# Attention block on one core: the output projection is evicted and added to x by one VectorE instruction

## The chip, the cores and the metric

The kernel is written in Bass for Trainium2 and runs on one core of one chip. The metric is the device time of one execution in microseconds (us). The kernel before takes 413.24 us, the median of 3 runs (413.13 to 413.28).

## What is computed

x has shape (4, 256, 32, 32): 4 images, 256 channels, 1024 pixels. Per image:

```
x_n = group_norm(x, gn_w, gn_b)                # 32 groups of 8 channels
q, k, v = conv1x1(x_n; wq,bq), conv1x1(x_n; wk,bk), conv1x1(x_n; wv,bv)
attn = softmax(q k^T * 64**-0.5)               # 4 heads of 64 channels, 1024 x 1024
out  = conv1x1(attn v; wp, bp)
return x + out
```

The change concerns the last two lines: the projection, its bias bp, and the addition of x.

## The kernel before

Each engine has its own instruction list, written out by hand; semaphores join them. An image is 32 slots (4 heads, 2 halves of the queries, 4 pairs of key tiles); the counter G runs over the 128 slots of four images and 13 more behind them (the tail). `place(G)` gives the image b and its slot g. Operands of full precision are split into two f16 parts, `hi` and `lo`.

In slot G, TensorE (PE) does `scores(G)` (two key tiles into one of two double banks st0, st1), two `maximum` matmuls for a later unit (banks mx0, mx1 in turn), at most one job of the table `JOBS`, and `weigh(G-4)`, the 24 products with v in bank pv. All jobs share one bank, `gen`. Before a job writes it, `bank_empty` waits until the job before has been evicted. The jobs are k, q, v (projections of the normalised image), o (transposes of the attention output), y (the output projection, one of four quarters: channel half i, pixel half j), mean and var (group statistics).

```
JOBS = {0: ("k", 1, 1, 0), 1: ("y", 0, 0, -1), 2: ("q", 1, 1, 0), 3: ("y", 1, 0, -1), 4: ("mean", 0, 0, 1),
        5: ("o", 1, 1, -1), 7: ("y", 0, 1, -1), 8: ("var", 0, 0, 1), 9: ("y", 1, 1, -1), 10: ("v", 1, 0, 0), ...}
TAIL_JOBS = {0: ("y", 0, 0, -1), 2: ("y", 1, 0, -1), 4: ("o", 1, 1, -1), 5: ("y", 0, 1, -1), 6: ("y", 1, 1, -1)}
```

The last number is the image relative to b: the y jobs of an image run in slots 1, 3, 7 and 9 of the next one, and those of image 3 in the tail. The first image thus has no y job, and the last has no mean and no var job. Where a long job (k, q, v, y) falls into a slot with the transpose of the maxima (every slot g with g mod 4 = 2), `early` puts it ahead of that transpose and of the first maximum.

What the other engines do in slot G:

- ScalarE (ACT): `exponent(G)`, two passes over the scores (L628 to p_hi, L631 to the full value), and behind it the eviction of the job of slot G. For y that is L617: scale, bias bp, into y32, and it raises s_y.
- VectorE (DVE), in this order: `normalise` (L717, L718) where g mod 4 = 0, `p_low(G-1)` (L711) for even G-1, `row_out` (L693) where g mod 4 = 2, the two row maxima (L681) with the low part of a v or o job (L705) around them, `join_max` (L686) where g mod 4 = 1, and the channel statistics of the next image (L727, L728) in slots 0 and 2 (1 and 3 in image 0). In the tail it also does `residual` (L735), in the slot behind that of the y job.
- GpSimd (POOL): the hi and lo parts of k and q (L853, L289), `p_low(G-1)` (L863) for odd G-1, and up to slot 128 the `residual` of the y job of slot G-1 (L858), which adds xres (a second load of x) to y32.
- The SP queue issues the loads, the copies of k and q to their operand tiles, the row of maxima (L325), the load of xres in slot 27 (L349) and the stores (L330), which wait for s_yx, raised by `residual`.

Of the kernel before, what the change touches and what calls it, by code (L numbers as in the profile page):

```python
# [12 lines left out]
def attention_block(nc, x, gn_w, gn_b, wq, bq, wk, bk, wv, bv, wp, bp, out):  # L13
# [55 lines left out]
    with ctx:  # L69
# [120 lines left out]
        s_pv = sem("s_pv")  # L190
        s_o32 = sem("s_o32")

        s_y = sem("s_y")
        s_yx = sem("s_yx")
        s_out = sem("s_out")
        s_ones = sem("s_ones")
# [198 lines left out]
        def _(pe):  # L395
            held = []

            def bank_empty():

                if not held:  # L400
                    return
                kind, i, j, b = held.pop()
                if kind in "kq":
                    wait(pe, s_e32[kind], nth(i, j, b) + 1)
                elif kind in "vo":
                    wait(pe, s_lo[kind], nth(i, j, b) + 1)
                elif kind == "y":
                    wait(pe, s_y, 4 * b + i + 2 * j + 1)
                else:
                    wait(pe, {"mean": s_gmean, "var": s_gvar}[kind], b + 1)  # L410

# [8 lines left out]
            def job(kind, i, j, b, bank=gen):  # L420
                if kind in "kqv":
                    wait_z(pe, b, j)
                if kind == "mean":
                    wait(pe, s_mv, b + 1)
                if kind == "var":
                    wait(pe, s_dev, b + 1)
                if kind == "o":
                    wait(pe, s_o32, UNITS * b + 4 * i + 2 * j + 2)
                if kind == "y":
                    wait(pe, s_lo["o"], nth(1, j, b) + 1)  # L430
                if bank is gen:
                    bank_empty()
                half = halves(j)
                o = slice(i * P, (i + 1) * P)
                if kind in "kq":
                    for mm in parts(bank[:, :], lambda t: (w_hi[kind][:, t, o], w_lo[kind][:, t, o]),
                                    lambda t: (z_hi[:, t, half], z_lo[:, t, half])):
                        last = mm
                if kind == "v":
                    for c in range(4):  # L440
                        k = slice((4 * j + c) * P, (4 * j + c + 1) * P)
                        for mm in parts(bank[:, c * P:(c + 1) * P], lambda t: (z_hi[:, t, k], z_lo[:, t, k]),
                                        lambda t: (w_hi["v"][:, t, o], w_lo["v"][:, t, o]), first=c == 0):
                            last = mm
                if kind == "y":
                    for mm in parts(bank[:, :], lambda t: (w_hi["p"][:, t, o], w_lo["p"][:, t, o]),
                                    lambda t: (oT_hi[:, t, half], oT_lo[:, t, half])):
                        last = mm
                if kind == "o":
                    for q in range(QT):  # L450
                        last = nc.tensor.transpose(bank[:, q * P:(q + 1) * P], o32[:, j, q, :], ident[:, :])  # L451
                if kind == "mean":
                    last = nc.tensor.matmul(bank[:, 0:CT], group_avg[:, :], mv[:, :, 0], start=True, stop=True)
                if kind == "var":
                    last = nc.tensor.matmul(bank[:, 0:CT], group_avg[:, :], dev2[:, :], start=True, stop=True)
                last.then_inc(s_gen_full, 1)
                if bank is gen:
                    held.append((kind, i, j, b))

# [131 lines left out]
        def _(act):  # L591
# [9 lines left out]
                act.wait_ge(s_gen_full, filled[0])  # L601

            def job(kind, i, j, b, bank=gen):
                bank_full()
                if kind in "kq":
                    wait(act, s_lo[kind], nth(i, j, b) - 1)
                    nc.scalar.activation(e32[kind][:, j, :], bank[:, :], ACT.Identity, bias=bias_s[kind][:, i:i + 1],  # L607
                                         scale=QKV_SCALE / (Z_SCALE * W_SCALE)).then_inc(s_e32[kind], 1)
                if kind == "v":
                    nc.scalar.activation(v_rows(v_hi, i, j), bank[:, :].rearrange("p (n d) -> p n d", d=D), ACT.Copy,  # L610
                                         scale=QKV_SCALE / (Z_SCALE * W_SCALE)).then_inc(s_hi["v"], 1)
                if kind == "o":
                    nc.scalar.activation(oT_hi[:, i, halves(j)], bank[:, :], ACT.Identity, bias=bv_o[:, i:i + 1])\
                      .then_inc(s_hi["o"], 1)
                if kind == "y":
                    wait(act, s_out, 64 * b)
                    nc.scalar.activation(y32[:, i, halves(j)], bank[:, :], ACT.Identity,  # L617
                                         bias=vec["p"][:, i:i + 1], scale=1.0 / (O_SCALE * W_SCALE)).then_inc(s_y, 1)
                if kind == "mean":
                    nc.scalar.activation(gmean[:, :], bank[:, 0:CT], ACT.Copy).then_inc(s_gmean, 1)  # L620
                if kind == "var":
                    nc.scalar.activation(gvar[:, :], bank[:, 0:CT], ACT.Copy).then_inc(s_gvar, 1)
# [50 lines left out]
        def _(dve):  # L673
# [55 lines left out]
                if t == CT - 1:  # L729
                    ins.then_inc(s_mv, 1)  # L730

            def residual(i, j, b):
                wait(dve, s_y, 4 * b + i + 2 * j + 1)
                wait(dve, s_xres, 16 * (b + 1))
                nc.vector.tensor_tensor(y32[:, i, halves(j)], y32[:, i, halves(j)], xres[:, i, halves(j)], ALU.add)\  # L735
                  .then_inc(s_yx, 1)

            def slot(G):
                b, g = place(G)
# [3 lines left out]
                    normalise(old // SPU)  # L743
                done, top = shift_at(G), maxima_at(G)
                early = done is not None and long_at(G)
                if slot_of(G - 1) is not None and lo_on_dve(G - 1):
                    p_low(G - 1)
                U, n = top or (None, None)
                todo = job_at(G - 1)
                if early and todo and todo[0] in "vo":  # L750
                    low(*todo)
                if done is not None:
# [2 lines left out]
                    row_max(U, n)  # L755
                if not early and todo and todo[0] in "vo":
                    low(*todo)
                if todo and todo[0] == "y" and G > TOTAL:
                    residual(*todo[1:])
                if top:  # L760
                    row_max(U, n + 1)
                if top and n == 2 * QT - 2:
# [65 lines left out]
        def _(pool):  # L828
# [23 lines left out]
                    wait(pool, s_mx_full, MXJ + 4)  # L852
                nc.gpsimd.tensor_copy(kq_hi[kind][:, halves(j)], e32[kind][:, j, :]).then_inc(s_hi[kind], 1)  # L853

            def residual(i, j, b):
                wait(pool, s_y, 4 * b + i + 2 * j + 1)
                wait(pool, s_xres, 16 * (b + 1))
                nc.gpsimd.tensor_tensor(y32[:, i, halves(j)], y32[:, i, halves(j)], xres[:, i, halves(j)], ALU.add)\  # L858
                  .then_inc(s_yx, 1)

            def p_low(G):
                wait(pool, s_exp, G + 1)
# [3 lines left out]
            def slot(G):  # L866
# [4 lines left out]
                    low_kq(pool, *todo)  # L871
                if slot_of(G - 1) is not None and not lo_on_dve(G - 1):
                    p_low(G - 1)
                if todo and todo[0] == "y" and G <= TOTAL:
                    residual(*todo[1:])
                if todo and todo[0] == "mean":
                    about_group_mean(pool, b + 1)
                if todo and todo[0] == "var":
                    norm_factors(b + 1)
                if b + 1 < B and g in (14, 15):  # L880
                    z_low(pool, b + 1, g - 14)

            nc.gpsimd.memset(ident[:, :], 0.0).then_inc(s_cfill, 1)
            nc.gpsimd.memset(group_avg[:, :], 1.0 / GROUP).then_inc(s_cfill, 1)
# [53 lines left out]
```

## Time and profile before

| | before |
|---|---|
| median of 3 runs | 413.24 us |
| profiled execution | 414.99 us |
| its span | 413.3 us |
| mean granted TensorE clock | 0.986 |
| TensorE matmul busy | 378.1 us, 91% |
| VectorE busy | 313.4 us, 76% |
| ScalarE busy | 313.4 us, 76% |
| GpSimd busy | 232.1 us, 56% |

The span is the profiled program from its first to its last instruction or transfer; the profiled execution's time has 1.7 us more around it. A busy share is an average over all stages. In the timeline, the first number is an instruction's start in us from the start of the span and the second its duration; a bracket tells how long the engine had been idle and whose work ended that.

### The profile page before, as it was taken

Reading aid. Unit: us, or ns where it says so; the run is one execution under the profiler, and the core shown is the slowest. Engines: PE = TensorE matmul, PEld = TensorE weight load, DVE = VectorE, ACT = ScalarE, POOL = GpSimd, SP = SyncE. Lnnn points to the kernel's source line nnn. Section 1 sums busy time; section 2 is a strip of 40 time slices with the busy share of each in tenths; the row PEclk is TensorE's granted clock in tenths of the full one; section 3 lists DMA queues with packets and bytes.
Section 4 is the critical chain, followed back from the end, with each engine's and each line's share of the span. In section 5 each row is a group of like instructions: output and inputs, shape, how many; then the busy total and the mean of one; then the engine's idle time right before and its main releaser. Section 6 shows DMA issues by size and latency. Waiting matters only on the chain.

```text
span 413.3 us, 11152 instructions
## 1 busy us (share of the span) xinstructions
PE 378.1 (91%) x4653; PEld 234.8 (57%) x4653; DVE 313.4 (76%) x536; ACT 313.4 (76%) x366; POOL 232.1 (56%) x195
## 2 busy tenths in 40 slices
PE   2789899899999999799999999799999999999884
PEld 1524476456665567456665657456665656655661
DVE  4776979678877987767878987757887687998552
ACT  1526787987878777988787787978778787888851
POOL 5144754776277665677476666478455744344440
PEclk9998999999999999999999999989999999999997
DMA  6054500034300611034320621003320351000301
GB/s 204 0 117 140 135 22 2 18 112 96 113 26 2 156 52 52 2 103 104 71 84 2 141 67 52 2 2 79 78 103 2 72 136 52 2 2 2 105 34 69
DMA packets 14409, 26.97 MB, mean 65 GB/s; under 512 B 2444, under 2 KB 4248, under 8 KB 14360
## 3 DMA queue, kind: packets, MB, share of 16 engines
q1 hardware_dynamic: 14336, 26.26, 22.9%
q8 instruction: 37, 0.61, 0.6%
q14 instruction: 12, 0.10, 0.1%
q10 hardware_dynamic: 24, 0.01, 0.0%
HBM read 9.44 MB, written 4.19 MB: 33 GB/s over the span
## 4 chain that ended last, share of the span: by engine, by line
PE 71%; DVE 15%; ACT 5%; issue 5%; DVEq 1%; POOLq 1%; POOL 1%
PE gen L417 17%; PE st L487 11%; PE st L488 10%; PE mx L465 10%; PE pv L505 6%; PE pv L508 6%; PE pv L507 6%; DVE mx L681 5%; DVE p_lo L711 4%; PE st L417 2%; ACT st L631 2%; DVEq L676 1%; DVE shift_row L693 1%; PE gen L451 1%; PE mx L472 1%
## 5 line engine op out<-in xcount | busy, mean ns | idle before, releaser
L863 POOL TENSOR_TENSOR p_lo<-p,p_hi 128x1024 f16<-128x1024 f32 x64 | 136.2, 2128 | 101.4 <-ACT p L631 101.4
L681 DVE TENSOR_REDUCE mx<-mx 128x1 f32<-128x512 f32 x256 | 171.3, 685 | 22.3 <-PE mx L465 19.6
L628 ACT ACTIVATE p_hi<-st 128x1024 f16<-128x1024 f32 x128 | 131.0, 1024 | 64.6 <-PE st L488 63.1
L505 PE MATMUL pv<-v_hi,p_hi 128*128 128x65 f16 x1024 | 106.1, 194 | 2.1 <-DVE o L718 1.8
L507 PE MATMUL pv<-v_lo,p_hi 128*128 128x64 f16 x1024 | 106.2, 193 | 0.0
L508 PE MATMUL pv<-v_hi,p_lo 128*128 128x65 f16 x1024 | 106.2, 194 | 0.0
L487 PE MATMUL st<-q_twice,k_both 128*128 128x512 f16 x256 | 97.6, 381 | 6.3 <-DVE p_lo L711 6.3
L505 PEld LDWEIGHTS pv<-v_hi,p_hi 128*128 128x128 f16 x1024 | 94.6, 98 | 12.0 <-issue 4.0
L507 PEld LDWEIGHTS pv<-v_lo,p_hi 128*128 128x128 f16 x1024 | 93.9, 98 | 13.2
L488 PE MATMUL st<-q_max,k_one 65*128 65x512 f16 x256 | 97.7, 382 | 0.0
L508 PEld LDWEIGHTS pv<-v_hi,p_lo 128*128 128x128 f16 x1024 | 94.0, 98 | 0.0
L465 PE MATMUL mx<-k_both,q_twice 128*128 128x512 f16 x244 | 87.8, 381 | 4.7 <-DVE shift_row L693 2.7
L711 DVE TENSOR_TENSOR p_lo<-st,p_hi 128x1024 f16<-128x1024 f32 x64 | 77.7, 1215 | 18.7 <-ACT st L631 18.5
L631 ACT ACTIVATE st<-st 128x1024 f32<-128x1024 f32 x64 | 65.3, 1021 | 0.0
L631 ACT ACTIVATE p<-st 128x1024 f32<-128x1024 f32 x64 | 65.3, 1020 | 0.0
L465 PEld LDWEIGHTS mx<-k_both,q_twice 128*128 128x128 f16 x244 | 24.2, 99 | 34.6 <-DVE shift_row L693 8.5
L487 PEld LDWEIGHTS st<-q_twice,k_both 128*128 128x128 f16 x256 | 25.2, 99 | 24.7 <-issue 5.8
L488 PEld LDWEIGHTS st<-q_max,k_one 65*128 65x128 f16 x256 | 25.1, 98 | 17.0 <-issue 0.3
L693 DVE TENSOR_SCALAR shift_row<-mx 4x128 f16<-4x128 f32 x32 | 8.9, 277 | 30.8 <-PE mx L472 30.8
L853 POOL CAST st_hi_k<-e_k 128x512 f16<-128x512 f32 x16 | 9.8, 610 | 32.0 <-ACT e_k L607 22.1
L417 PE MATMUL gen<-w_hi_v,z_lo 128*128 128x128 f16 x128 | 23.4, 225 | 0.0
L417 PE MATMUL gen<-w_lo_v,z_hi 128*128 128x128 f16 x128 | 23.4, 225 | 0.0
(140 smaller groups left out, 491.6 us busy)
## 6 DMA issues: line engine op xcount, KB each, us to landing
xres<-in_x_dram SPq DMA_DIRECT2D x4, 1024.0 KB, 5.0
out_dram<-y SPq DMA_DIRECT2D x16, 256.0 KB, 2.2
q_twice<-st_hi_q SPq DMA_DIRECT2D x28, 128.0 KB, 2.3
xin<-in_x_dram SPq DMA_DIRECT2D x6, 512.0 KB, 3.3
k_both<-st_hi_k SPq DMA_DIRECT2D x16, 128.0 KB, 2.3
k_one<-st_hi_k SPq DMA_DIRECT2D x16, 128.0 KB, 2.4
k_both<-st_lo_k SPq DMA_DIRECT2D x16, 128.0 KB, 2.3
q_max<-st_lo_q SPq DMA_DIRECT2D x14, 128.0 KB, 2.4
```

What stands on the lines that cost most here:

```text
L417: yield nc.tensor.matmul(dst, a, c, start=first and t == 0 and n == 0, stop=t == CT - 1 and n == 2, skip_group_check=True)
L465: nc.tensor.matmul(mxb[(MXJ * U + j) % 2][:, :], q_twice[:, head, q:q + P], k_both[:, head, halves(part)], start=True, stop=True).then_inc ...
L487: nc.tensor.matmul(dst, k_both[:, head, k], q_twice[:, head, q], start=True, stop=False)
L488: last = nc.tensor.matmul(dst, k_one[:, head, k], q_max[:, head, q], start=False, stop=True)
L505: nc.tensor.matmul(pv_v[:, q, :], hi, vh, start=k == 0 and q == 0, stop=False, skip_group_check=True)
L507: nc.tensor.matmul(pv_v[:, q, 0:D], hi, vl, start=False, stop=False, skip_group_check=True)
L508: last = nc.tensor.matmul(pv_v[:, q, :], lo, vh, start=False, stop=k == NK - 1, skip_group_check=True)
L628: nc.scalar.activation(p_hi[:, G % PR, :, :], scores, ACT.Exp, scale=SM_SCALE / M_SCALE)
L631: nc.scalar.activation(p_full(G), scores, ACT.Exp, scale=SM_SCALE / M_SCALE).then_inc(s_exp, 1)
L681: nc.vector.reduce_max(mx8[:, U % 2, tile, part:part + 1], mxb[(MXJ * U + j) % 2][:, :], AX.X)\
L711: nc.vector.tensor_tensor(p_lo[:, G % PR, :, :], p_full(G), p_hi[:, G % PR, :, :], ALU.subtract)\
L863: nc.gpsimd.tensor_tensor(p_lo[:, G % PR, :, :], p_full(G), p_hi[:, G % PR, :, :], ALU.subtract)\
```

## The change

ScalarE no longer evicts y jobs, and they no longer raise s_gen_full but a semaphore of their own, s_y_full. On VectorE `finish` takes the place of `residual`: one scalar_tensor_tensor reads the bank and xres, computes bank * scale + xres, writes y32 and raises s_yx. It stands in the slot behind that of the y job, for all 16 quarters, ahead of `p_low`, `row_out` and the maxima and behind `normalise`. TensorE's `bank_empty` waits for s_yx instead of s_y. On GpSimd `residual` goes, and `add_bias` adds bp to xres in place, 128 x 1024 elements each in slots 29 and 31 of every image. The load of xres stays where it is.

```diff
--- before.py
+++ after.py
@@ -190,7 +190,8 @@
         s_pv = sem("s_pv")
         s_o32 = sem("s_o32")
 
-        s_y = sem("s_y")
+        s_y_full = sem("s_y_full")
+        s_xb = sem("s_xb")
         s_yx = sem("s_yx")
         s_out = sem("s_out")
         s_ones = sem("s_ones")
@@ -405,7 +406,7 @@
                 elif kind in "vo":
                     wait(pe, s_lo[kind], nth(i, j, b) + 1)
                 elif kind == "y":
-                    wait(pe, s_y, 4 * b + i + 2 * j + 1)
+                    wait(pe, s_yx, 4 * b + i + 2 * j + 1)
                 else:
                     wait(pe, {"mean": s_gmean, "var": s_gvar}[kind], b + 1)
 
@@ -453,7 +454,7 @@
                     last = nc.tensor.matmul(bank[:, 0:CT], group_avg[:, :], mv[:, :, 0], start=True, stop=True)
                 if kind == "var":
                     last = nc.tensor.matmul(bank[:, 0:CT], group_avg[:, :], dev2[:, :], start=True, stop=True)
-                last.then_inc(s_gen_full, 1)
+                last.then_inc(s_y_full if kind == "y" else s_gen_full, 1)
                 if bank is gen:
                     held.append((kind, i, j, b))
 
@@ -601,6 +602,8 @@
                 act.wait_ge(s_gen_full, filled[0])
 
             def job(kind, i, j, b, bank=gen):
+                if kind == "y":
+                    return
                 bank_full()
                 if kind in "kq":
                     wait(act, s_lo[kind], nth(i, j, b) - 1)
@@ -612,10 +615,6 @@
                 if kind == "o":
                     nc.scalar.activation(oT_hi[:, i, halves(j)], bank[:, :], ACT.Identity, bias=bv_o[:, i:i + 1])\
                       .then_inc(s_hi["o"], 1)
-                if kind == "y":
-                    wait(act, s_out, 64 * b)
-                    nc.scalar.activation(y32[:, i, halves(j)], bank[:, :], ACT.Identity,
-                                         bias=vec["p"][:, i:i + 1], scale=1.0 / (O_SCALE * W_SCALE)).then_inc(s_y, 1)
                 if kind == "mean":
                     nc.scalar.activation(gmean[:, :], bank[:, 0:CT], ACT.Copy).then_inc(s_gmean, 1)
                 if kind == "var":
@@ -729,11 +728,14 @@
                 if t == CT - 1:
                     ins.then_inc(s_mv, 1)
 
-            def residual(i, j, b):
-                wait(dve, s_y, 4 * b + i + 2 * j + 1)
-                wait(dve, s_xres, 16 * (b + 1))
-                nc.vector.tensor_tensor(y32[:, i, halves(j)], y32[:, i, halves(j)], xres[:, i, halves(j)], ALU.add)\
-                  .then_inc(s_yx, 1)
+            def finish(i, j, b, bank):
+
+                wait(dve, s_y_full, 4 * b + i + 2 * j + 1)
+                wait(dve, s_xb, CT * b + i + 1)
+                wait(dve, s_out, 64 * b)
+                nc.vector.scalar_tensor_tensor(out=y32[:, i, halves(j)], in0=bank[:, :],
+                                               scalar=1.0 / (O_SCALE * W_SCALE), in1=xres[:, i, halves(j)],
+                                               op0=ALU.mult, op1=ALU.add).then_inc(s_yx, 1)
 
             def slot(G):
                 b, g = place(G)
@@ -743,10 +745,12 @@
                     normalise(old // SPU)
                 done, top = shift_at(G), maxima_at(G)
                 early = done is not None and long_at(G)
+                todo = job_at(G - 1)
+                if todo and todo[0] == "y":
+                    finish(*todo[1:], tail_bank(G - 1))
                 if slot_of(G - 1) is not None and lo_on_dve(G - 1):
                     p_low(G - 1)
                 U, n = top or (None, None)
-                todo = job_at(G - 1)
                 if early and todo and todo[0] in "vo":
                     low(*todo)
                 if done is not None:
@@ -755,8 +759,6 @@
                     row_max(U, n)
                 if not early and todo and todo[0] in "vo":
                     low(*todo)
-                if todo and todo[0] == "y" and G > TOTAL:
-                    residual(*todo[1:])
                 if top:
                     row_max(U, n + 1)
                 if top and n == 2 * QT - 2:
@@ -852,11 +854,10 @@
                     wait(pool, s_mx_full, MXJ + 4)
                 nc.gpsimd.tensor_copy(kq_hi[kind][:, halves(j)], e32[kind][:, j, :]).then_inc(s_hi[kind], 1)
 
-            def residual(i, j, b):
-                wait(pool, s_y, 4 * b + i + 2 * j + 1)
+            def add_bias(b, i):
                 wait(pool, s_xres, 16 * (b + 1))
-                nc.gpsimd.tensor_tensor(y32[:, i, halves(j)], y32[:, i, halves(j)], xres[:, i, halves(j)], ALU.add)\
-                  .then_inc(s_yx, 1)
+                nc.gpsimd.tensor_scalar(xres[:, i, :], xres[:, i, :], vec["p"][:, i:i + 1], None, ALU.add)\
+                  .then_inc(s_xb, 1)
 
             def p_low(G):
                 wait(pool, s_exp, G + 1)
@@ -871,14 +872,14 @@
                     low_kq(pool, *todo)
                 if slot_of(G - 1) is not None and not lo_on_dve(G - 1):
                     p_low(G - 1)
-                if todo and todo[0] == "y" and G <= TOTAL:
-                    residual(*todo[1:])
                 if todo and todo[0] == "mean":
                     about_group_mean(pool, b + 1)
                 if todo and todo[0] == "var":
                     norm_factors(b + 1)
                 if b + 1 < B and g in (14, 15):
                     z_low(pool, b + 1, g - 14)
+                if b < B and g in (29, 31):
+                    add_bias(b, (g - 29) // 2)
 
             nc.gpsimd.memset(ident[:, :], 0.0).then_inc(s_cfill, 1)
             nc.gpsimd.memset(group_avg[:, :], 1.0 / GROUP).then_inc(s_cfill, 1)
```

On VectorE, the piece from the maxima of slot 1 to slot 4 of the image behind the first one (y is y32, mx is a mx bank or mx8), before:

```order
L681 TENSOR_REDUCE mx<-mx 128x1 x2
L686 TENSOR_REDUCE mx<-mx 128x4
L693 TENSOR_SCALAR shift_row<-mx 4x128
L681 TENSOR_REDUCE mx<-mx 128x1 x2
L727 BN_STATS bn<-xin 128x6 x2
L728 BN_AGGR mv<-bn 128x2
L711 TENSOR_TENSOR p_lo<-st,p_hi 128x1024
L681 TENSOR_REDUCE mx<-mx 128x1 x2
L717 RECIPROCAL rden<-pv 128x4
L718 TENSOR_TENSOR o<-pv,rden 128x4x64
L681 TENSOR_REDUCE mx<-mx 128x1 x2
```

and now:

```order
L680 TENSOR_REDUCE mx<-mx 128x1 x2
L685 TENSOR_REDUCE mx<-mx 128x4
L736 SCALAR_TENSOR_TENSOR y<-gen,xres 128x512
L692 TENSOR_SCALAR shift_row<-mx 4x128
L680 TENSOR_REDUCE mx<-mx 128x1 x2
L726 BN_STATS bn<-xin 128x6 x2
L727 BN_AGGR mv<-bn 128x2
L710 TENSOR_TENSOR p_lo<-st,p_hi 128x1024
L680 TENSOR_REDUCE mx<-mx 128x1 x2
L716 RECIPROCAL rden<-pv 128x4
L717 TENSOR_TENSOR o<-pv,rden 128x4x64
L736 SCALAR_TENSOR_TENSOR y<-gen,xres 128x512
```

The first `L736` stands between the joined maxima of slot 1 and the shift_row of slot 2, the second behind o, ahead of the maxima of slot 4.

```order
L680 TENSOR_REDUCE mx<-mx 128x1 x2
L716 RECIPROCAL rden<-pv 128x4
L717 TENSOR_TENSOR o<-pv,rden 128x4x64
L736 SCALAR_TENSOR_TENSOR y<-gen,xres 128x512
L680 TENSOR_REDUCE mx<-mx 128x1 x2
L710 TENSOR_TENSOR p_lo<-st,p_hi 128x1024
L680 TENSOR_REDUCE mx<-mx 128x1 x2
L685 TENSOR_REDUCE mx<-mx 128x4
L736 SCALAR_TENSOR_TENSOR y<-gen,xres 128x512
```

This is the same list on VectorE at slots 8 to 10 now: the third `L736` follows o, the fourth the joined maxima.

On GpSimd, slots 29 to 31 of image 0 and the first three slots behind them, before:

```order
L853 CAST st_hi_q<-e_q 128x512
L289 TENSOR_TENSOR st_lo_q<-e_q,st_hi_q 128x512
L863 TENSOR_TENSOR p_lo<-p,p_hi 128x1024 x2
L853 CAST st_hi_k<-e_k 128x512
L289 TENSOR_TENSOR st_lo_k<-e_k,st_hi_k 128x512
L863 TENSOR_TENSOR p_lo<-p,p_hi 128x1024
L858 TENSOR_TENSOR y<-y,xres 128x512
L853 CAST st_hi_q<-e_q 128x512
L289 TENSOR_TENSOR st_lo_q<-e_q,st_hi_q 128x512
```

and now:

```order
L855 CAST st_hi_q<-e_q 128x512
L290 TENSOR_TENSOR st_lo_q<-e_q,st_hi_q 128x512
L859 TENSOR_SCALAR xres<-xres,vec_cols 128x1024
L864 TENSOR_TENSOR p_lo<-p,p_hi 128x1024
L859 TENSOR_SCALAR xres<-xres,vec_cols 128x1024
L864 TENSOR_TENSOR p_lo<-p,p_hi 128x1024
L855 CAST st_hi_k<-e_k 128x512
L290 TENSOR_TENSOR st_lo_k<-e_k,st_hi_k 128x512
L864 TENSOR_TENSOR p_lo<-p,p_hi 128x1024
L855 CAST st_hi_q<-e_q 128x512
```

Two passes over xres have come in, one ahead of each p_lo, and the two residual additions have gone.

## Rows read from the trace of the kernel before

**Rows 1.** The page, busy time of each engine, share of the span, instructions.

```profile
PE 378.1 (91%) x4653; PEld 234.8 (57%) x4653; DVE 313.4 (76%) x536; ACT 313.4 (76%) x366; POOL 232.1 (56%) x195
```

**Rows 2.** Timeline, ScalarE, VectorE, TensorE around slot 2 of image 1; start, duration.

```profile
130.21 0.69 ACT L617 ACTIVATE y<-gen,vec_cols 128x512 f32<-128x512 f32 x1
...
131.45 0.16 DVE L686 TENSOR_REDUCE mx<-mx 128x4 f32<-128x8 f32 x1
133.12 0.28 DVE L693 TENSOR_SCALAR shift_row<-mx 4x128 f16<-4x128 f32 x1 [1.52 <-PE mx L472]
...
131.52 0.38 PE L417 MATMUL gen<-z_hi,w_hi_q 128*128 128x512 f16 x1
```

**Rows 3.** Groups by line and form: count, busy time, mean ns, idle before.

```profile
L863 POOL TENSOR_TENSOR p_lo<-p,p_hi 128x1024 f16<-128x1024 f32 x64 | 136.2, 2128 | 101.4 <-ACT p L631 101.4
...
L858 POOL TENSOR_TENSOR y<-y,xres 128x512 f32<-128x512 f32 x12 | 15.2, 1266 | 0.0
...
L705 DVE SCALAR_TENSOR_TENSOR oT_lo<-gen,bv_o,oT_hi 128x512 f16<-128x512 f32 x16 | 11.9, 743 | 2.7 <-ACT oT_hi L613 2.7
...
L705 DVE SCALAR_TENSOR_TENSOR v_lo<-gen,v_hi 128x512 f16<-128x512 f32 x16 | 10.9, 681 | 2.6 <-ACT v_hi L610 2.6
...
L853 POOL CAST st_hi_k<-e_k 128x512 f16<-128x512 f32 x16 | 9.8, 610 | 32.0 <-ACT e_k L607 22.1 <-SPq L387 9.9
```

**Rows 4.** Timeline, VectorE and TensorE, slots 3 and 4 of image 1.

```profile
136.55 1.17 DVE L711 TENSOR_TENSOR p_lo<-st,p_hi 128x1024 f16<-128x1024 f32 x1
...
139.08 0.42 DVE L718 TENSOR_TENSOR o<-pv,rden 128x256 f32<-128x256 f32 x1
139.42 1.28 DVE L681 TENSOR_REDUCE mx<-mx 128x1 f32<-128x512 f32 x2
...
137.87 0.38 PE L487 MATMUL st<-q_twice,k_both 128*128 128x512 f16 x1 [0.28 <-DVE p_lo L711]
...
138.95 0.28 PE L453 MATMUL gen<-mv,group_avg 128*128 128x2 f32 x2
```

**Rows 5.** Timeline, VectorE and TensorE, slots 8 to 10 of image 1.

```profile
149.04 0.42 DVE L718 TENSOR_TENSOR o<-pv,rden 128x256 f32<-128x256 f32 x1
...
154.28 0.16 DVE L686 TENSOR_REDUCE mx<-mx 128x4 f32<-128x8 f32 x1
...
149.67 0.28 PE L455 MATMUL gen<-dev,group_avg 128*128 128x2 f32 x2
...
154.95 0.22 PE L417 MATMUL gen<-w_hi_v,z_hi 128*128 128x128 f16 x1
```

**Rows 6.** Timeline, VectorE, slot 1 of image 2.

```profile
225.96 0.16 DVE L686 TENSOR_REDUCE mx<-mx 128x4 f32<-128x8 f32 x1
```

**Rows 7.** Timeline, VectorE and TensorE, slots 1, 2, 9 and 10 of image 3.

```profile
321.19 0.16 DVE L686 TENSOR_REDUCE mx<-mx 128x4 f32<-128x8 f32 x1
...
344.04 0.16 DVE L686 TENSOR_REDUCE mx<-mx 128x4 f32<-128x8 f32 x1
...
321.86 0.38 PE L417 MATMUL gen<-z_hi,w_hi_q 128*128 128x512 f16 x1
...
344.71 0.22 PE L417 MATMUL gen<-w_hi_v,z_hi 128*128 128x128 f16 x1
```

**Rows 8.** Timeline, VectorE and ScalarE, the tail.

```profile
397.95 2.14 DVE L735 TENSOR_TENSOR y<-y,xres 128x512 f32<-128x512 f32 x1 [0.61 <-ACT y L617]
...
410.14 0.69 DVE L735 TENSOR_TENSOR y<-y,xres 128x512 f32<-128x512 f32 x1 [1.44 <-ACT y L617]
...
409.42 0.69 ACT L617 ACTIVATE y<-st,vec_cols 128x512 f32<-128x512 f32 x1 [1.45 <-PE st L417]
```

**Rows 9.** Timeline, GpSimd, slots 30 and 32 of image 0 (p_lo of 29 and 31).

```profile
119.99 2.12 POOL L863 TENSOR_TENSOR p_lo<-p,p_hi 128x1024 f16<-128x1024 f32 x1 [0.37 <-ACT p L631]
124.93 2.13 POOL L863 TENSOR_TENSOR p_lo<-p,p_hi 128x1024 f16<-128x1024 f32 x1 [2.81 <-ACT p L631]
```

**Rows 10.** The page, DMA issues: count, KB each, median us to landing.

```profile
xres<-in_x_dram SPq DMA_DIRECT2D x4, 1024.0 KB, 5.0
```

## The prediction

> **What bounds the kernel now.** I read the busy times first: TensorE's matmuls fill 91% of the span, VectorE and ScalarE 76% each, GpSimd 56% [rows 1]. By these averages, 0.7 us moved from ScalarE to VectorE now and then is neutral. But TensorE sets the pace: VectorE waits for it at slot 2 with all its work done [rows 2], and GpSimd idles 101.4 us for ScalarE, which has its scores from TensorE [rows 3]. So what counts is whether TensorE gets its bank back in time. I therefore went to the timeline around each y job and asked two things: when does TensorE want bank gen again, and when will VectorE have emptied it?
>
> Around slot 2 of image 1 [rows 2] ScalarE evicts y from 130.21 to 130.90, and TensorE starts the next job in gen, q, at 131.52. So there are 0.62 us to spare. VectorE ends its joined maxima at 131.61 and then sits idle for 1.52 us until TensorE's transpose arrives. That idle time looks like cover, but it isn't: the transpose stands behind the q job on TensorE, and the q job will now wait for VectorE.
>
> **What the eviction costs on VectorE.** No row before shows the new instruction. The nearest has the same operation, a PSUM bank and an SBUF tile as inputs, 512 elements and a constant scale: the low part of v, 681 ns; the form with a scale per partition takes 743 ns [rows 3]. I take 0.68 us and keep 0.74 for the range.
>
> From VectorE's end to TensorE's start I take 0.15 us: p_lo ends at 136.55 + 1.17 = 137.72, and TensorE, which waited for it, starts at 137.87 [rows 4]. A following VectorE instruction starts some 0.08 us ahead of the profiled end of the one before it: o ends at 139.50, the maxima start at 139.42 [rows 4].
>
> **The waits, one by one, image 1.** In each, the new instruction starts 0.08 us ahead of the end of its predecessor, takes 0.68, and TensorE follows 0.15 later.
>
> - Slot 2: predecessor is the joined maximum, end 131.61 [rows 2]. The eviction runs from 131.53 to 132.21, TensorE starts q at 132.36 instead of 131.52: 0.84 us. Everything behind it, transpose, shift row, statistics, p_lo of slot 3 and the 0.28 us that TensorE waits for that p_lo [rows 4], moves along unchanged, since VectorE's next instruction waits for TensorE too.
> - Slot 4: VectorE reaches the eviction only behind the statistics, p_lo, two maxima and normalise. o ends at 139.50; eviction 139.42 to 140.10, TensorE 140.25. It wanted the bank for the mean job at 138.95 [rows 4]: 1.30 us. This is the largest, because VectorE is without idle time from slot 2's second maximum to here.
> - Slot 8: o ends at 149.46, eviction to 150.06, TensorE 150.21 instead of 149.67 for the var job [rows 5]: 0.54 us.
> - Slot 10: joined maximum ends at 154.44, eviction to 155.04, TensorE 155.19 instead of 154.95 for v [rows 5]: 0.24 us.
>
> Together 2.92 us. Image 2 repeats image 1 about 94.51 us later (the joined maximum of slot 1 is at 225.96 instead of 131.45 [rows 2, 6]), so it costs 2.92 too. In image 3 VectorE has no statistics to take and TensorE no mean and no var job; the next user of gen comes one or more slots later, and only slots 2 and 10 are left: 321.35 gives 322.10 against 321.86, and 344.20 gives 344.95 against 344.71 [rows 7], 0.24 us each, 0.48 us. Image 0 has no y job. Sum of the waits: 2.92 + 2.92 + 0.48 = 6.32 us. They lie on the path whole, because behind slot 10 VectorE and ScalarE again wait for TensorE and nothing runs on a clock of its own that could catch up.
>
> **What is saved.** ScalarE loses 16 evictions of 0.69 us, but after those in the images it waits for TensorE anyway: nothing. GpSimd loses 12 additions of 1.27 us [rows 3]: nothing on the path, since it idles 101.4 us for ScalarE ahead of its p_lo [rows 3]. In the tail the last quarter goes through ScalarE (409.42 to 410.11) and VectorE (410.14 to 410.83) before it can be stored [rows 8]; one instruction of 0.68 replaces both: 1.41 - 0.68 = 0.73 us less. The first addition of the tail, 2.14 us instead of 0.69 [rows 8], has nobody waiting: both quarters' stores are far from the end, and the next normalise comes later.
>
> **What is added on GpSimd.** A pass over 1024 elements with one input costs between twice the 512-element cast, 1.22 us, and the two-input 1024 pass, 2.13 us [rows 3]; I take 1.3. The first comes ahead of a p_lo with 0.37 us idle before it, the second ahead of one with 2.81 us [rows 9], so one p_lo is late by about 0.9 us (1.8 at the upper end). TensorE uses that p_lo four slots behind its scores: hidden. If that cover were gone, it would be 0.9 us per image. xres lands 5.0 us after its issue in slot 27 [rows 10], which is about when slot 29's pass comes up. The SP queue keeps its order; s_yx comes earlier for the stores, never later than the queue itself.
>
> **The sum.** 6.32 - 0.73 = 5.6 us more. The profiled execution takes 414.99 us (span 413.3 and 1.7 around it) and would take 420.6. It stands 1.75 us above the median; the same shift on the median 413.24 gives 418.8.
>
> **A rule against the change.** The rows say that both engines are 76% busy and that VectorE is without idle time just where two evictions now go. The Trainium skill's Perfetto Trace Analysis (Optimizing Scalar/DVE Operations) says that where the vector engine is saturated, work may better be moved to ScalarE, the opposite of this change. By busy shares alone it would see no saturation here and charge nothing; by stage, as I read it, the price is the one above.
>
> **The rivals.**
>
> *VectorE is blocked by GpSimd.* The addition at 397.95 took 2.14 us and not 0.69, beside GpSimd's last p_lo [rows 8]. If the new instruction, which reads xres from SBUF too, met the same, each of the ten waits could grow by 1.45 us: 5.6 + 14.5, 433.3 us. Against it: VectorE's low parts of v and o read a bank and an SBUF tile beside GpSimd's p_lo and average 681 and 743 ns [rows 3]. The Trainium skill's page SBUF — State Buffer (Who interferes with whom) says that a VectorE instruction with two SBUF inputs contends with a GpSimd instruction that reads SBUF, and one with at most one doesn't; the new one has one, so by it this rival is void. Chance 0.05.
>
> *Only part of the waits is felt.* If TensorE's own short waits around slots 2, 8 and 10 swallow the new ones and slot 4 alone stays: 2 x 1.30 - 0.73 = +1.9, 415.1 us. Against it: only 0.28 us of waiting is seen near there. Chance 0.14.
>
> *All hidden.* If VectorE ran ahead of my walk by the time of slot 4's wait, only the tail's gain is left: -0.73, 412.5 us, within the 0.2% (0.8 us) that a measurement can tell from no change. Chance 0.05. It is also what comes out if TensorE's pace has slack that the rows don't show.
>
> *Faster: the blocked addition was on the path.* If the evictions are hidden and the 2.14 us addition of the tail held up the end, its 1.45 us come back as well: 413.24 - 0.73 - 1.45 = 411.1 us. It decides from the point where every eviction ends 0.15 us ahead of TensorE's next job in gen. Against it: in slot 4 that is missed by 1.30 us. Chance 0.04.
>
> **How the numbers follow.** The forecast as walked through has 0.72. Upper bound of its own: ten evictions at 0.74 and no overlap with the predecessor, (0.06 + 0.08) x 10 = 1.4 us, 420.2; with the late GpSimd p_lo felt once, 421.0. Low end: the partial case, 415.1. The range 415.1 to 421.0 leaves out the hidden, the faster and the blocked case. Slower by over 0.2%: 0.72 + 0.14 + 0.05 = 0.91; within 0.2%: 0.05; faster: 0.04.
>
> **What would show it.** In the changed profile TensorE waits for VectorE's eviction, most often and longest ahead of the mean job (1.3 us in images 1 and 2) and of q (0.8), less ahead of var and v, and only little in image 3. The eviction takes about 0.68 us also beside GpSimd. The distance from image 1 to image 2 grows from 94.5 to about 97.4 us. It would be wrong if TensorE's waits ahead of those four jobs are absent, if the eviction takes over 1 us, or if waits elsewhere shrink by as much.

## The result and the profile after

| | before | changed |
|---|---|---|
| median | 413.26 us (413.13 to 413.92, 4 runs) | 419.46 us (416.11 to 423.01, 4 runs) |
| ratio | 1 | 1.012, 95% interval 1.006 to 1.018 |
| profiled execution | 414.99 us, span 413.3 | 419.48 us, span 417.7 |

Two runs in this document lie over 1.5% above the fastest of their kernel, 423.01 us here and 490.41 us in the experiment on the tail, and are left out of the ratios and of every reading of the clock; without the first the changed kernel's median is 419.43 us.

The change makes the kernel slower, by about what was forecast (418.8 us). The page's busy times after:

```profile
PE 378.5 (91%) x4653; PEld 233.5 (56%) x4653; DVE 319.2 (76%) x548; ACT 304.0 (73%) x350; POOL 239.7 (57%) x191
```

Against [rows 1] ScalarE has lost 9.4 us of work and VectorE gained 5.8; the shares hardly move. The averages say nothing of the 4.4 us that the span has grown by. TensorE's waits do. From the waits of the changed kernel (engine and line, released by: us in total, times, longest):

```profile
PE gen L454 <- DVE y L736: 2.3, 2, 1.1
...
PE gen L418 <- DVE y L736: 1.4, 2, 0.7
...
PE gen L456 <- DVE y L736: 0.7, 2, 0.4
```

Three new kinds of wait, two times each: the mean job, the q job and the var job of images 1 and 2, all for the bank that the eviction L736 holds. Before there was none of them. The v job in slot 10 is late too, by 0.25 us in image 1, but so little that no wait is listed for it. The timeline of the changed kernel around slots 1 to 4 of image 1, VectorE first, then TensorE, then GpSimd:

```profile
132.09 0.16 DVE L685 TENSOR_REDUCE mx<-mx 128x4 f32<-128x8 f32 x1
132.17 0.69 DVE L736 SCALAR_TENSOR_TENSOR y<-gen,xres 128x512 f32<-128x512 f32 x1
134.60 0.28 DVE L692 TENSOR_SCALAR shift_row<-mx 4x128 f16<-4x128 f32 x1 [1.75 <-PE mx L473]
...
140.90 0.68 DVE L736 SCALAR_TENSOR_TENSOR y<-gen,xres 128x512 f32<-128x512 f32 x1
...
133.00 0.38 PE L418 MATMUL gen<-z_hi,w_hi_q 128*128 128x512 f16 x1 [0.68 <-DVE y L736]
...
139.35 0.38 PE L488 MATMUL st<-q_twice,k_both 128*128 128x512 f16 x1 [0.29 <-DVE p_lo L710]
...
141.73 0.35 PE L454 MATMUL gen<-mv,group_avg 128*128 128x2 f32 x2 [1.13 <-DVE y L736]
...
131.89 2.13 POOL L864 TENSOR_TENSOR p_lo<-p,p_hi 128x1024 f16<-128x1024 f32 x1
```

This trace reached image 1 0.64 us later than the one before (joined maxima at 132.09 instead of 131.45). Taking that off, q starts at 132.36, to the hundredth where the forecast had put it; the shift_row that follows is 0.84 us late, although VectorE is idle for 1.75 us ahead of it. The eviction of slot 4 starts at 140.90 - 0.64 - 0.84 = 139.42, again as forecast, and the old wait of 0.28 us for p_lo is still there. The bracket counts only from the modelled end of the matmul before, so the wait costs a little more than it shows: 0.84 us where 0.68 stands.

**Where 4.4 us of span come from.** The joined maxima of a unit (8 values into 4) recur at fixed places of every image and make a good ruler. Those of slot 13 in the trace of before (those of slot 1 are in [rows 2, 6, 7]):

```profile
166.42 0.16 DVE L686 TENSOR_REDUCE mx<-mx 128x4 f32<-128x8 f32 x1
...
260.93 0.16 DVE L686 TENSOR_REDUCE mx<-mx 128x4 f32<-128x8 f32 x1
...
356.18 0.16 DVE L686 TENSOR_REDUCE mx<-mx 128x4 f32<-128x8 f32 x1
```

and those of slots 1 and 13 of the changed kernel:

```profile
169.82 0.16 DVE L685 TENSOR_REDUCE mx<-mx 128x4 f32<-128x8 f32 x1
...
230.68 0.16 DVE L685 TENSOR_REDUCE mx<-mx 128x4 f32<-128x8 f32 x1
...
268.47 0.16 DVE L685 TENSOR_REDUCE mx<-mx 128x4 f32<-128x8 f32 x1
...
327.41 0.16 DVE L685 TENSOR_REDUCE mx<-mx 128x4 f32<-128x8 f32 x1
...
362.92 0.16 DVE L685 TENSOR_REDUCE mx<-mx 128x4 f32<-128x8 f32 x1
```

| stretch | before, us | changed, us | difference |
|---|---|---|---|
| start to slot 1 of image 1 | 131.45 | 132.09 | +0.64 |
| image 1, slots 1 to 13 | 34.97 | 37.73 | +2.76 |
| image 1 slot 13 to image 2 slot 1 | 59.54 | 60.86 | +1.32 |
| image 2, slots 1 to 13 | 34.97 | 37.79 | +2.82 |
| image 2 slot 13 to image 3 slot 1 | 60.26 | 58.94 | -1.32 |
| image 3, slots 1 to 13 | 34.99 | 35.51 | +0.52 |
| from there to the end | 57.1 | 54.8 | -2.3 |

The 0.64 us ahead of slot 1 of image 1 are less than this stretch varies by from trace to trace: in the changed kernel once more and in the one without GpSimd's passes, both below, slot 1 comes at 129.81 and at 131.79 us.

The slots with y jobs cost 2.76 + 2.82 + 0.52 = 6.10 us. The two 1.32 us, of opposite sign, come from the clock: in each trace TensorE was granted less than its full clock once between two images, only in different ones. Windows of before, then of the changed kernel (columns: busy time of PE, PEld, DVE, ACT, POOL, granted clock, DMA share, GB/s):

```profile
264.00:276.00 12.00, 10.11 (x100) 5.49 (x99) 7.46 (x12) 10.47 (x12) 6.97 (x5) 0.86 0.01 1
404.00:412.00 8.00, 4.44 (x12) 1.53 (x12) 2.13 (x3) 1.39 (x3) 0.00 (x0) 0.79 0.12 47
```

```profile
176.00:184.00 8.00, 7.20 (x67) 3.92 (x66) 5.20 (x10) 6.73 (x8) 4.86 (x4) 0.79 0.21 66
404.00:416.00 12.00, 7.89 (x118) 5.14 (x118) 4.11 (x8) 0.77 (x2) 3.75 (x2) 1.00 0.17 67
```

The tail of before ran partly at the lower level of 1.2 GHz (0.79 on average in its last projections), that of the changed kernel at full clock. The tail after:

```profile
413.29 0.69 DVE L736 SCALAR_TENSOR_TENSOR y<-gen,xres 128x512 f32<-128x512 f32 x1 [1.64 <-PE gen L418]
414.59 0.69 DVE L736 SCALAR_TENSOR_TENSOR y<-st,xres 128x512 f32<-128x512 f32 x1 [0.60 <-PE st L418]
```

The last quarter's eviction starts 5.17 us later than ScalarE's did (409.42 [rows 8]), but the profiled execution ends only 4.49 us later (419.48 against 414.99): the merged instruction saves 0.7 us. (The spans, 413.3 and 417.7, are rounded too coarsely for this.) The rest of the tail's difference, about 1.6 us, is the clock of the last twelve matmuls: from the start of the first to that of the last it is 4.06 us before and 2.37 us now.

### The profile page after: what moved, and what is told of

The parts are those of the page before. It is cut to its first block, busy times and chain, and to the rows that moved or that the text cites. A ratio compares the mean times of both kernels' runs of the same rounds, so it can differ in the third digit from the quotient of the medians.

```text
span 417.7 us, 11132 instructions
## 1 busy us (share of the span) xinstructions
PE 378.5 (91%) x4653; PEld 233.5 (56%) x4653; DVE 319.2 (76%) x548; ACT 304.0 (73%) x350; POOL 239.7 (57%) x191
## 4 chain that ended last, share of the span: by engine, by line
PE 67%; DVE 18%; issue 5%; ACT 5%; DVEq 2%; POOLq 1%; POOL 1%
PE gen L418 16%; PE st L488 10%; PE st L489 9%; PE mx L466 9%; PE pv L506 6%; DVE mx L680 6%; PE pv L509 6%; PE pv L508 6%; DVE p_lo L710 5%; PE st L418 2%; DVEq L675 2%; ACT st L630 2%; DVE y L736 1%; DVE bn L726 1%; DVE shift_row L692 1%
## 5 line engine op out<-in xcount | busy, mean ns | idle before, releaser
L627 ACT ACTIVATE p_hi<-st 128x1024 f16<-128x1024 f32 x128 | 131.0, 1024 | 76.9 <-PE st L489 75.5
L859 POOL TENSOR_SCALAR xres<-xres,vec_cols 128x1024 f32<-128x1024 f32 x8 | 22.8, 2848 | 0.1
L418 PE MATMUL gen<-w_hi_v,z_hi 128*128 128x128 f16 x128 | 22.2, 219 | 0.3
```

The costliest lines, as they stand in the source:

```text
L418: yield nc.tensor.matmul(dst, a, c, start=first and t == 0 and n == 0, stop=t == CT - 1 and n == 2, skip_group_check=True)
L627: nc.scalar.activation(p_hi[:, G % PR, :, :], scores, ACT.Exp, scale=SM_SCALE / M_SCALE)
```

## Experiments

The comparisons below were run on a chip where the kernel before takes 415.1 us (first four) and 414.6 us (last four), with a spread of some 5 us that follows the granted clock; so ratios are wide and the ruler above, read in stretches at full clock, carries the verdicts. "Distance" is from the joined maxima of slot 1 of one image to those of the next; before it is 94.51 us from image 1 to image 2. That of the changed kernel is 98.59 us with a fall of the clock in it, and 97.3 us without it: its own 37.73 for slots 1 to 13 and the 59.54 that the rest takes before, at full clock. The diffs show the lines that matter; declarations and what "..." stands for are left out.

**The changed kernel once more.** No edit.

> The changed kernel once more, to see how far its time spreads and whether the spread goes with the granted clock (four runs so far: 416.11 us at a mean clock of 0.999, 419.43 and 419.48 at 0.99, 423.01 at 0.98). My theory, waits for the bank: 2.8 us more per image in images 1 and 2, 0.5 in image 3, 0.8 less in the tail, the same in every run, and the rest of the spread is the clock, about 3.4 us for each 0.01 of mean clock. Rival, the spread is in the waits: then the distance between the joined maxima of slot 1 of images 2 and 3 differs from 96.7 us although the clock between them is 1.00.

Measured: 418.22 us (415.69 to 421.47, 8 runs), ratio 1.009 (1.006 to 1.012). Eleven runs of the changed kernel, these and three of the result, by mean clock: 421.47 at 0.982, 419.97 at 0.986, 419.4 to 419.5 at 0.990 and 0.991, 418.6 at 0.992, 417.6 to 417.9 at 0.996, 415.7 to 416.5 at 0.999. The spread goes with the clock, 3.1 us per 0.01 by a straight line through them. The kernel before has the same slope, 3.0: 42 runs from 416.5 at 0.982 to 411.5 at 0.994. At 0.990 its nine runs take 413.1 to 413.9 us, median 413.6, and the changed kernel's three at 0.990 and 0.991 take 419.4 to 419.5: 5.8 us, the size of the change at equal clock. The changed kernel was granted 0.993 on average, the one before 0.986, which hides some 2 us of it in these medians; why it gets the better clock isn't settled. In this run's trace both distances (98.26 and 98.03) have a fall of the clock in them, so the test of 96.7 us at full clock couldn't be read here; slots 1 to 13 of image 1 take 37.72 us again (37.73), and the three kinds of wait are the same to 0.1 us.

**Without GpSimd's passes.**

```diff
-                wait(dve, s_xb, CT * b + i + 1)
+                wait(dve, s_xres, 16 * (b + 1))
...
-                if b < B and g in (29, 31):
-                    add_bias(b, (g - 29) // 2)
```

> The changed kernel without GpSimd's two passes over xres per image; the bias bp is left out of the result. My theory: GpSimd's p_lo of slot 29 comes 2.85 us earlier, nobody waits for it, time as the changed kernel at the same granted clock (416.1 us at 0.999, 419.5 at 0.99), and the waits for L736's bank unchanged at 1.1 us (mean), 0.7 (q), 0.4 (var). Rival, the pass is on the path: up to 2.85 us less per image, 408 to 413 us.

Measured: 419.48 us (416.93 to 419.88, 6 runs), ratio 1.010 (1.007 to 1.013); 419.3 and 419.6 at a clock of 0.991, where the changed kernel has 419.4. Distance 97.26 us at full clock, as the changed kernel's 97.3. The passes cost nothing on the path, as forecast, though each takes far longer than I had bounded it. From the groups of the changed kernel:

```profile
L859 POOL TENSOR_SCALAR xres<-xres,vec_cols 128x1024 f32<-128x1024 f32 x8 | 22.8, 2848 | 0.1
```

and its timeline around slots 29 to 31 of image 0:

```profile
120.26 2.85 POOL L859 TENSOR_SCALAR xres<-xres,vec_cols 128x1024 f32<-128x1024 f32 x1
123.08 2.13 POOL L864 TENSOR_TENSOR p_lo<-p,p_hi 128x1024 f16<-128x1024 f32 x1
125.19 2.85 POOL L859 TENSOR_SCALAR xres<-xres,vec_cols 128x1024 f32<-128x1024 f32 x1
128.00 2.13 POOL L864 TENSOR_TENSOR p_lo<-p,p_hi 128x1024 f16<-128x1024 f32 x1
```

Both p_lo of [rows 9] are some 2.4 us late (after the 0.64 us of this trace's start), and TensorE, which uses them four slots behind the scores, doesn't wait for either.

**The mean job two slots later.**

```diff
-JOBS = {..., 4: ("mean", 0, 0, 1), 5: ("o", 1, 1, -1), 7: ...
+JOBS = {..., 5: ("o", 1, 1, -1), 6: ("mean", 0, 0, 1), 7: ...
```

> The changed kernel with the mean job moved from slot 4 to slot 6 of images 1 and 2 (image 0 has it there already); VectorE does the same work. My theory, only the moment of the release counts: the wait of 1.13 us ahead of the mean job goes in two images, net 1.1 us each since a hidden wait of 0.3 us for normalise comes back, so 2.2 us less than the changed kernel at the same clock, 413.9 us at 0.999 or 417.3 at 0.99. Rival, VectorE's added load counts wherever it is waited for: no change, the wait shows up ahead of o or the scores instead.

Measured: 421.49 us (419.40 to 423.41, 6 runs), ratio 1.016 (1.013 to 1.019): slower than the changed kernel, the opposite of my expectation. Distance from image 1 to image 2 98.07 us, all at full clock: 0.8 more than the changed kernel's 97.3, where 1.1 less were expected. The wait ahead of mean for y has gone, but another has taken its place:

```profile
PE gen L454 <- DVE oT_lo L704: 3.1, 2, 1.5
```

In slot 6 the job ahead of mean is o, whose bank is also released by VectorE, by L704, behind shift_row and a maximum of slot 6:

```profile
144.37 0.28 DVE L692 TENSOR_SCALAR shift_row<-mx 4x128 f16<-4x128 f32 x1 [0.45 <-PE mx L473]
144.59 0.69 DVE L680 TENSOR_REDUCE mx<-mx 128x1 f32<-128x512 f32 x1
145.20 0.74 DVE L704 SCALAR_TENSOR_TENSOR oT_lo<-gen,bv_o,oT_hi 128x512 f16<-128x512 f32 x1
```

L704 ends at 145.94 and mean starts at 146.08 after 1.53 us of waiting, 0.4 more than for y. I had looked at who follows y and not at who then precedes mean. The run doesn't tell my theory from the rival as planned, since it created a new late release; it does show the same mechanism with another instruction.

**The new eviction in the tail alone.**

```diff
                 elif kind == "y":
-                    wait(pe, s_y, 4 * b + i + 2 * j + 1)
+                    wait(pe, s_y if b < B - 1 else s_yx, 4 * b + i + 2 * j + 1)
...
-                residual(*todo[1:])
+                finish(*todo[1:], tail_bank(G - 1))
...
+                if b == B - 1 and g in (29, 31):
+                    add_bias((g - 29) // 2)
```

> The kernel before, with the new eviction for the four quarters of the last image alone (in the tail), and GpSimd's passes over xres in image 3 alone. My theory: images 1 to 3 as before, the tail 0.77 us shorter: 412.5 us if the granted clock falls as before (ratio 0.998), and no wait for L617's or the new eviction inside the images. Rival, the tail's gain was only a clock effect: 413.3 us, ratio 1.000.

Measured: 414.36 us (12 runs; 412.56 to 416.17 without the one at 490.41), ratio 0.9989 (0.9968 to 1.0011). By itself that is no difference, and at equal clock it is little more: 412.6 to 413.4 at 0.991 against 413.6 before at 0.990, 413.7 to 414.4 at 0.987 against 414.6 at 0.986, where 0.001 of clock alone is worth 0.3 us. Distance 94.51, as before, and TensorE waits for no eviction inside the images. The trace shows the gain itself. Its last quarter:

```profile
407.70 0.69 DVE L740 SCALAR_TENSOR_TENSOR y<-st,xres 128x512 f32<-128x512 f32 x1 [0.89 <-PE st L419]
```

From the start of the last eviction to the end of the profiled execution it is 414.99 - 409.42 = 5.57 us before, 419.48 - 414.59 = 4.89 in the changed kernel and 412.56 - 407.70 = 4.86 here: 0.7 us less in both. The 0.77 us of the expectation took the rounded spans for exact.

**Two evictions instead of one, released by the second.**

```diff
+                if b < B - 1:
+                    nc.vector.scalar_tensor_tensor(out=again[:, :], in0=bank[:, :],
+                                                   scalar=1.0 / (O_SCALE * W_SCALE), in1=xres[:, i, halves(j)],
+                                                   op0=ALU.mult, op1=ALU.add)
                 nc.vector.scalar_tensor_tensor(out=y32[:, i, halves(j)], in0=bank[:, :],
```

> The changed kernel, with every eviction inside images 1 to 3 done twice on VectorE, first into a tile that nobody reads, then into y32; the bank is released by the second. 0.60 us more VectorE work ahead of each release. My theory: each wait that exists grows by 0.60 us, four in images 1 and 2, two in image 3; from the joined maxima of slot 1 of one image to those of the next 97.3 + 2.4 = 99.7 us at full clock; about 6 us over the changed kernel in all. Rival, the changed kernel's loss is something other than the late release (the clock, GpSimd's passes): the distance stays near 97.3 us.

Measured: 427.98 us (427.94 to 428.72, 3 runs), ratio 1.032 (1.028 to 1.037). Its waits:

```profile
PE gen L419 <- DVE y L741: 5.5, 6, 1.3
PE gen L455 <- DVE y L741: 3.5, 2, 1.7
...
PE gen L457 <- DVE y L741: 1.9, 2, 1.0
```

Ahead of mean 1.7 instead of 1.1 us, ahead of var 1.0 instead of 0.4, ahead of q 1.3 instead of 0.7, and q and v together now six times and not two: each grew by 0.6. At full clock only image 3 can be read: slots 1 to 13 take 36.94 us (334.11 to 371.05) instead of 35.51, 1.4 us more for its two waits, where 1.2 were expected. The distances, 102.6 and 101.9 us, hold two falls of the clock each; at 1.3 us apiece they leave 100.0 and 99.3, about the 99.7 of the expectation. In all, 427.9 us at 0.984 is some 6.6 us over the changed kernel at that clock (an estimate: 419.4 at 0.990 and 3.1 us per 0.01), where about 6 were expected.

**The same extra work, but behind the release.**

```diff
                                                op0=ALU.mult, op1=ALU.add).then_inc(s_yx, 1)
+                if b < B - 1:
+                    nc.vector.bn_stats(extra[:, :], w_in["p"][:, :, :].rearrange("p t c -> p (t c)"))
```

> The changed kernel, with 0.60 us of VectorE work put behind each eviction inside images 1 to 3 (statistics of a constant tile into a tile that nobody reads), so that the bank is released as before and only VectorE's load grows. My theory: slots 2 and 10 hide it in the idle time ahead of shift_row, slots 4 and 8 pass on little: 0.2 to 0.6 us per image, distance from image to image 97.5 to 97.9 us. Rival, VectorE's load is the bound: the same 2.4 us per image as with two evictions, 99.7 us.

Measured: 420.02 us (419.89 to 420.80, 3 runs), ratio 1.013 (1.009 to 1.017). From its groups of waits and its timeline around slot 4:

```profile
PE gen L455 <- DVE y L737: 2.3, 2, 1.1
...
PE gen L457 <- DVE y L737: 0.7, 2, 0.4
```

```profile
141.16 0.68 DVE L737 SCALAR_TENSOR_TENSOR y<-gen,xres 128x512 f32<-128x512 f32 x1
141.76 0.68 DVE L741 BATCH_NORM_STATS2 extra<-w_in_p 128x6 f32<-128x512 f32 x1
142.36 1.27 DVE L681 TENSOR_REDUCE mx<-mx 128x1 f32<-128x512 f32 x2
```

The waits are those of the changed kernel, but for a third short one ahead of q or v. Slots 1 to 13 of image 1 take 37.72 us (changed: 37.73), the distance from image 2 to image 3, at full clock, is 96.72 (changed: 96.73); image 3's slots 35.72 (35.51). Twelve extra instructions of 0.68 us cost 0.2 us in the stretches that can be read, less than I expected, and the same work ahead of the release costs 1.4 us in image 3 alone. The run times are less kind: 419.9 and 420.0 at 0.992, where the one run of the changed kernel at 0.992 takes 418.6. But the two profiled executions differ by 0.54 us only (420.02 and 419.48), 0.26 of it ahead of the first extra instruction, with the falls of the clock in the same stretches and yet mean clocks of 0.992 and 0.990; so equal mean clocks don't resolve 1 us. Even at 1.4 us it is far from the 6.6 of the two evictions. VectorE's load is not the bound; the moment of the release is.

**The statistics ahead of shift_row.**

```diff
+                if b + 1 < B and b > 0 and g == 2:
+                    channel_stats(b + 1, 1)
                 if done is not None:
                     row_out(done)
...
-                if b + 1 < B and g in ((1, 3) if b == 0 else (0, 2)):
+                if b + 1 < B and g in ((1, 3) if b == 0 else (0,)):
```

> The changed kernel with the channel statistics of slot 2 (1.64 us, images 1 and 2) moved ahead of shift_row, into the 1.75 us in which VectorE waits for TensorE. My theory: the eviction in slot 4 starts 0.9 to 1.1 us earlier, TensorE's wait ahead of the mean job falls from 1.13 to 0.2 to 0.4 us, its wait of 0.29 us for p_lo goes: 1.1 to 1.2 us less per image, distance 97.3 - 1.15 = 96.1 us, 2.3 us less in all at the same clock. Rival, the wait ahead of mean has another cause than VectorE's backlog from the statistics: distance stays 97.3 us.

Measured: 414.82 us (413.26 to 416.77, 10 runs), ratio 1.001 (0.998 to 1.004); at a clock of 0.991 416.8 us, at 0.999 413.3 to 414.5 (changed: 419.4 and 415.7 to 416.5). Its timeline, VectorE in slots 2 to 4 and TensorE's mean job:

```profile
131.58 0.69 DVE L736 SCALAR_TENSOR_TENSOR y<-gen,xres 128x512 f32<-128x512 f32 x1
132.19 1.45 DVE L726 BATCH_NORM_STATS2 bn<-xin 128x6 f32<-128x512 f32 x2
133.71 0.21 DVE L727 BATCH_NORM_AGGREGATE mv<-bn 128x2 f32<-128x12 f32 x1
134.02 0.28 DVE L692 TENSOR_SCALAR shift_row<-mx 4x128 f16<-4x128 f32 x1
...
139.11 0.68 DVE L736 SCALAR_TENSOR_TENSOR y<-gen,xres 128x512 f32<-128x512 f32 x1
...
139.94 0.35 PE L454 MATMUL gen<-mv,group_avg 128*128 128x2 f32 x2 [0.38 <-DVE y L736]
```

The statistics fit into the idle time; shift_row is 2.52 us behind the joined maxima (changed: 2.51). The eviction of slot 4 comes 7.61 us behind them instead of 8.81, TensorE waits 0.38 instead of 1.13 us, and its wait for p_lo has gone. Distance 96.07 us: 1.2 less than 97.3, as expected. So the largest wait was VectorE's backlog, and two thirds of it were the statistics. Against the kernel before it is still slower: the ratio of 1.001 comes from the better clock (0.997 on average against 0.987), and at 0.991 and 0.990 it is 416.8 against 413.6 us.

**Both findings on the kernel before.** The tail's edit and the statistics' edit together.

> The kernel before with the new eviction in the tail alone and with the statistics of slot 2 ahead of shift_row in images 1 and 2. My theory: the tail gives 0.77 us as in tail_only; TensorE's wait of 0.28 us for p_lo and the hidden one of 0.3 us for normalise go in images 1 and 2, distance 94.51 - 0.5 = 94.0 us; 1.7 to 1.9 us less than before in all, ratio 0.9955. Rival, shift_row comes late by the statistics and gives it back: distance 94.5 us, ratio 0.998.

Measured: 413.03 us (409.04 to 414.73, 12 runs) against 414.63 before on the same chip: ratio 0.9952 (0.9917 to 0.9986). Slots 1 to 13 of image 1 take 34.52 us (130.60 to 165.12) instead of 34.97. By clock: 411.6 to 412.8 us at 0.991 against 413.6 before at 0.990, and 413.3 to 414.0 at 0.987 against 414.6 at 0.986. It beats both kernels, but part of the ratio is again the clock (0.990 on average against 0.987): at equal clock, by straight lines through the runs, the gain is some 0.7 to 0.9 us, less than the 1.7 to 1.9 expected. The terms in the trace are 2 x 0.45 us for the statistics and, by the experiment on the tail, 0.7 us there, 1.6 us in all; why the run times give back less stays open.

## Why the prediction was right

- **Who sets the pace, and that VectorE's idle time is no cover.** Confirmed: in slot 2 VectorE idles for 1.75 us behind an eviction that TensorE waited for, and 12 extra instructions behind the releases cost 0.2 us in the stretches at full clock, while 12 ahead of them cost some 6.6 us.
- **The price of the eviction, 0.68 us.** Measured 680 to 692 ns over all 16, also beside GpSimd's p_lo: the eviction at 132.17 took 0.69 us within the p_lo of 131.89 to 134.02. The rival in which GpSimd blocks it falls. The Trainium skill's page SBUF — State Buffer (Who interferes with whom) says that a VectorE instruction with at most one SBUF input, outside its two-port modes, does not contend with GpSimd, and the trace agrees.
- **The waits, 2.92 us per image in images 1 and 2, 0.48 in image 3.** Measured 2.76, 2.82 and 0.52. Slot 2: 0.84, as forecast. Slot 4: mean is 1.30 us late, as forecast, and the maximum behind it 1.37, but TensorE gets some 0.3 us back right behind, so that the slot costs 1.08 in all: before, its weigh had a hidden wait for normalise in that slot (1.23 us from the maximum to the next scores, 0.94 after), which no bracket shows and I missed. Slot 8 cost 0.6 instead of 0.54, slot 10 0.25 instead of 0.24.
- **The tail, -0.73 us.** Measured -0.7, in two traces. The addition of 2.14 us, the point of the rival on the other side, was nobody's wait.
- **GpSimd's pass, 1.22 to 2.13 us.** Outside its bounds: 2.85. On GpSimd the addition of a per-partition value in place over 1024 f32 elements took longer than the two-input subtraction of the same size with f16 output, 2.13. Both p_lo are 2.4 us late and not one by 0.9. The cover I named held all the same, so the pass costs nothing on the path, as forecast, though its price was wrong.
- **Sum.** 6.32 - 0.73 = 5.6 forecast, 6.10 - 0.7 = 5.4 in the trace, 5.8 at equal clock. (The upper end of the range, 420.2 and 0.9 more, is 421.1 and not 421.0.) The Trainium skill's Perfetto Trace Analysis (Optimizing Scalar/DVE Operations) would offload work to ScalarE where VectorE is saturated. Here VectorE is 76% busy before and after, so its condition isn't met by load; moving the work to VectorE was still wrong, and the reason is its place in the queue.
- **What was left out.** The granted clock. With it single runs of the changed kernel moved from 415.7 to 421.5 us, as much as the whole sum; that the median met the forecast to 0.7 us is partly luck.

## To carry to other kernels

Where a shared PSUM bank is on the pace-setting engine's path, an eviction's cost is how far its end lies behind the moment at which the bank's next user wants it. That is set by when its engine's queue reaches it and by its own duration, and that engine's busy share tells neither: look for the next user of the bank and for everything that stands ahead of the eviction in the new queue, and after moving a job look also at the job that now precedes it. An engine's idle time counts as cover only if what ends it does not itself wait for the work put there. Work that releases nothing can go into such idle time, as the statistics did.

## What the runs showed of the hardware

- The granted clock falls in some stretches, and a run takes about 3.0 us more (before) or 3.1 us more (changed) per 0.01 of mean clock lost. Single executions of the same kernel differ in it: 0.982 to 0.994 before, 0.982 to 0.999 changed. At equal mean clock runs still differ by 0.8 us (413.1 to 413.9 at 0.990), while a stretch at full clock repeats to 0.01 us: slots 1 to 13 of image 1 take 37.73, 37.72, 37.73 and 37.72 us in the changed kernel, once more, without the passes, and with the work behind the release.
- GpSimd's tensor_scalar with a per-partition operand, 128 x 1024 f32 in place: 2.85 us, against 2.13 us for its tensor_tensor of that size with f16 output.
- VectorE's scalar_tensor_tensor from PSUM and SBUF f32 to SBUF f32, 512 elements: 0.68 to 0.69 us, also beside GpSimd; its tensor_tensor with both inputs in SBUF took 2.14 us once beside a GpSimd instruction and 0.69 the other three times, in the tail of the kernel before.
